# An attention block whose value products run for two key tiles at a time

## The reference, cut to what matters

```python
h = _layernorm(x) * (1 + ca) + sa                    # x: (16, 1024, 256)
q = (h @ Wq.T).reshape(b, t, 8, 64)
kv_latent = h @ Wkv_down.T                           # (b, t, 64)
k = (kv_latent @ Wk_up.T).reshape(b, t, 8, 64)
v = (kv_latent @ Wv_up.T).reshape(b, t, 8, 64)
attn = softmax(einsum('bqhd,bkhd->bhqk', q, k) * 64 ** -0.5)
x = x + ga * (einsum('bhqk,bkhd->bqhd', attn, v) @ Wo.T)
h = _layernorm(x) * (1 + cb) + sb
x = x + gb * (h @ weight.T + pooled(h) @ disha)
```

## Time and profile before

| what | value |
|---|---|
| median of 3 runs | 3648.74 us (3648.51 to 3649.03) |
| the profiled execution | 3651.17 us, its span 3649.2 us |
| mean granted TensorE clock | 0.983 |
| PE / DVE / ACT / POOL busy | 97% / 67% / 46% / 69% |
| matmul records | 15014 |

### The profile page before, as it was taken

How to read it: one execution, slowest core, us unless ns; L and a number is a source line. 1 busy time by engine, 2 the same in 40 slices (tenths; PEclk the granted TensorE clock), 3 DMA queues, 4 the chain that set the end, 5 groups by cost and what they waited for, 6 DMA issues and landing times.

```text
span 3649.2 us, 50991 instructions
## 1 busy us (share of the span) xinstructions
PE 3530.1 (97%) x15014; PEld 1840.0 (50%) x15014; DVE 2446.3 (67%) x2846; ACT 1684.6 (46%) x3075; POOL 2515.4 (69%) x1513
## 2 busy tenths in 40 slices
PE   5999999999999999999999999999999999999997
PEld 3444555545454554545545455454555545555454
DVE  4667667676676767657676576766767667676663
ACT  1445445444454545445454354543545445454443
POOL 1677767676776767668677676866767677686775
PEclk7999999999999999999999999999999999999998
DMA  1101010010101001010010100101010010100101
GB/s 55 35 20 48 24 56 21 30 48 27 47 26 55 18 27 53 24 51 18 33 47 24 51 27 27 50 27 48 21 41 36 27 48 27 53 18 33 35 30 32
DMA packets 98076, 129.24 MB, mean 35 GB/s; under 512 B 11120, under 2 KB 62448, under 8 KB 97776
## 3 DMA queue, kind: packets, MB, share of 16 engines
q1 hardware_dynamic: 97776, 125.64, 9.9%
HBM read 41.11 MB, written 16.81 MB: 16 GB/s over the span
## 4 chain that ended last, share of the span: by engine, by line
PE 94%; DVE 3%; issue 2%; ACT 1%; POOL 0%; DMA 0%; SPq 0%; DVEq 0%; POOLq 0%; ACTq 0%
PE ps_mix L543 28%; PE ps_max L593 18%; PE ps_score L564 14%; PE ps_score L566 13%; PE ps_side_b L531 7%; PE ps_side_b L651 5%; PE ps_side_a L638 4%; PE ps_side_b L669 3%; PE ps_side_a L631 1%; PE ps_side_a L658 1%; DVE h_lo L972 1%; PE ps_side_a L608 0%; DVE recip L931 0%; DVE neg_max L950 0%; PE ps_side_a L622 0%
## 5 line engine op out<-in xcount | busy, mean ns | idle before, releaser
L811 POOL TENSOR_TENSOR prob_sum<-prob_sum,probs 128x1024 f32<-128x1024 f32 x768 | 1837.5, 2393 | 575.7 <-ACT probs L710 518.7
L950 DVE TENSOR_REDUCE neg_max<-ps_max 128x1 f32<-128x1024 f32 x1016 | 1243.5, 1224 | 721.1 <-PE ps_max L593 710.9
L710 ACT ACTIVATE probs<-ps_score 128x512 f32<-128x512 f32 x2048 | 1113.0, 596 | 1140.9 <-PE ps_score L566 1129.2
L543 PE MATMUL ps_mix<-probs,values 128*64 128x512 f32 x4096 | 1109.5, 620 | 0.0
L564 PE MATMUL ps_score<-query,key_hi 128*128 128x512 f32 x2048 | 839.8, 410 | 37.2 <-issue 35.8
L566 PE MATMUL ps_score<-query_m,key_lo 128*128 128x512 f32 x2048 | 810.2, 396 | 0.0
L593 PE MATMUL ps_max<-key_hi,query 128*128 128x512 f32 x2032 | 749.8, 450 | 5.1 <-DVE neg_max L950 5.0
L593 PEld LDWEIGHTS ps_max<-key_hi,query 128*128 128x128 f32 x2032 | 304.5, 189 | 830.4 <-issue 433.6
L811 POOL TENSOR_TENSOR prob_sum<-probs 128x1024 f32<-128x1024 f32 x128 | 305.5, 2387 | 457.7 <-ACT probs L710 457.7
L931 DVE RECIPROCAL recip<-recip 128x128 f32<-128x128 f32 x512 | 481.4, 942 | 17.8 <-ACT recip L761 17.8
L564 PEld LDWEIGHTS ps_score<-query,key_hi 128*128 128x128 f32 x2048 | 387.5, 189 | 155.2 <-issue 73.9
(11 more groups left out here) (115 smaller groups left out, 2701.8 us busy)
## 6 DMA issues: line engine op xcount, KB each, us to landing
query_m<-query SPq DMA_DIRECT2D x128, 512.0 KB, 3.2
x_in<-in_L_attn_x_dram SPq DMA_DIRECT2D x16, 1024.0 KB, 5.5
x_mid<-in_L_attn_x_dram SPq DMA_DIRECT2D x64, 256.0 KB, 6.9
out_dram<-x_mid SPq DMA_DIRECT2D x64, 256.0 KB, 2.2
h_t<-gates_scratch SPq DMA_DIRECT2D x16, 256.0 KB, 6.7
query_m<-max_row SPq DMA_DIRECT2D x128, 4.0 KB
mixed<-in_L_wmod_dram SPq DMA_DIRECT2D x1, 1536.0 KB, 11.3
mixed<-in_L_attn_Wq_dram SPq DMA_DIRECT2D x1, 512.0 KB, 4.9
```

The lines of the kernel that those rows point to most:

```text
L543: last = nc.tensor.matmul(ps_mix[g % 2][j * R:j * R + R, :], values[par][:, k, :], probs[:, s % RING, j * HALF:(j + 1) * HALF], start=(k = ...
L710: nc.scalar.activation(probs[:, s % RING, half * HALF:(half + 1) * HALF], ps_score[half], ACT.Exp, scale=SCALE).then_inc(exps_done, 1)
L811: nc.gpsimd.tensor_tensor(out=total[:, :], in0=before, in1=probs[:, s % RING, :], op=ALU.add).then_inc(adds_done, 1)
L950: nc.vector.tensor_reduce(neg_max[:, m:m + 1], z.max_bank(m, ps_max, ps_scores)[:, :], AX_X, ALU.max, negate=True).then_inc(maxima_done, 1)
```

## The change

`slot` on TensorE is cut into four functions, whose bodies are the old ones, and their order is new. Even steps run the scores, the side work but for the denominator, the maximum, then the mixes of the two steps before in one block, and the denominator right behind it. Odd steps run the scores, the maximum and the side work, and no mix. The mixes of the last two steps of a batch (62 and 63) run in step 0 of the next slot. As step 0, 2, 4 and 6 of each group are even, side work at k = 0, 2, 4 and 6 now stands ahead of the maximum, and the denominator behind two mixes. The lists of the other engines are as before.

```diff
+MIXED = 2
...
-                    if s == 0 and z.has_o:
-                        if not z.has_c:
-                            need(pe, exps_done, 2 * STEPS * z.c)
-                        zo = Slot(z.o, 1 - z.par)
-                        mix(zo, STEPS - 1)
-                    if s > 0 and z.has_c:
-                        if s == 1:
-                            need(pe, a_drained, values_drained(z))
-                        mix(z, s - 1)
...
+            def side_work(z, s, denominators):
+                for kind, i, bank, b, w in z.at(s):
+                    if (kind == "denominator") != denominators:
+                        continue
...
+            def mixes(z, s):
+                if s == 0 and z.has_o:
+                    if not z.has_c:
+                        need(pe, exps_done, 2 * STEPS * z.c)
+                    zo = Slot(z.o, 1 - z.par)
+                    for t in range(STEPS - MIXED, STEPS):
+                        mix(zo, t)
+                if s > 0 and z.has_c and s % MIXED == 0:
+                    if s == MIXED:
+                        need(pe, a_drained, values_drained(z))
+                    for t in range(s - MIXED, s):
+                        mix(z, t)
...
             def slot(z):
                 for s in range(STEPS):
+                    scores(z, s)
+                    if s % MIXED == 0:
+                        side_work(z, s, denominators=False)
+                        maximum(z, s)
+                        mixes(z, s)
+                        side_work(z, s, denominators=True)
+                    else:
+                        maximum(z, s)
+                        side_work(z, s, denominators=False)
```

More of the change, by code:

```diff
@@ L547, in mix, with scores @@
                     last.then_inc(group_done, 1)
+            def scores(z, s):
+                g, k = divmod(s, NT)
+                if z.has_c:
+                    if k == 0:
+                        need(pe, max_row_set, 16 * (GROUPS * z.c + g + 1))
+                    if s == 0:
+                        need(pe, key_row_set, 16 * (z.c + 1))
+                        if isinstance(z.c, int) and z.c == 0:
+                            pe.wait_ge(maxima_done, STEPS - MAX_LAG)
+                    for j in range(2):
+                        need(pe, exps_done, 2 * (STEPS * z.c + s) - 1 + j)
+                        nc.tensor.matmul(ps_score[j], key_hi[z.par][:, k * P:(k + 1) * P],
+                                         group_queries(g)[:, j, :], start=True, stop=False)
+                        nc.tensor.matmul(ps_score[j], key_lo[z.par][:, k * P:(k + 1) * P],
+                                         query_m[:, g % 2, j * HALF:(j + 1) * HALF],
+                                         start=False, stop=True).then_inc(scores_ready, 1)
@@ new lines, in maximum @@
+            def maximum(z, s):
+                item = z.max_item(s)
+                if item:
+                    b, m = item
+                    gm, unit = divmod(m, NT)
+                    hm, qt = 2 * (gm // 2) + unit // 4, 4 * (gm % 2) + unit % 4
+                    kpar = (1 - z.par) if s >= MAX_LAG else z.par
+                    if m % (2 * NT) == 0:
+                        made = ("query", gm + 1)
+                        here = made in [p[2:4] for p in z.lists[1] if (p[4] == 0) == (s < MAX_LAG)]
+                        need(pe, b_drained, z.through(1, *made) + 1 if here else z.before(1))
+                    need(pe, maxima_done, STEPS * b + m - (0 if z.has_c else 1))
+                    bank = z.max_bank(m, ps_max, ps_scores)
+                    for half in range(2):
+                        last = nc.tensor.matmul(bank[:, half * HALF:(half + 1) * HALF],
+                                                query[:, hm, qt * P:(qt + 1) * P],
+                                                key_hi[kpar][:, half * HALF:(half + 1) * HALF],
+                                                start=True, stop=True)
+                    last.then_inc(max_scores_ready, 1)
@@ L549, in slot @@
             def slot(z):
                 for s in range(STEPS):
[L551 to L568, removed]
@@ L569, in slot @@
-                    if s == 0 and z.has_o:
-                        if not z.has_c:
-                            need(pe, exps_done, 2 * STEPS * z.c)
-                        zo = Slot(z.o, 1 - z.par)
-                        mix(zo, STEPS - 1)
-                    if s > 0 and z.has_c:
-                        if s == 1:
-                            need(pe, a_drained, values_drained(z))
-                        mix(z, s - 1)
[L579 to L663, removed]
-                            need(pe, b_drained, count)
-                            products = [(hp, wp, f) for f in range(NF)
-                                        for hp, wp in ((h2_hi, w_ffn_hi), (h2_lo, w_ffn_hi), (h2_hi, w_ffn_lo))]
-                            for j in range(CT):
-                                for q, (hp, wp, f) in enumerate(products):
-                                    last = nc.tensor.matmul(side[:, j * D:(j + 1) * D], hp[:, f, j * P:(j + 1) * P],
-                                                            wp[:, f, :], start=(q == 0), stop=(q == len(products) - 1))
-                        last.then_inc(full[bank], 1)
```

70 lines of the change are left out of this document (added).

## The result

The changed kernel takes 3990.9 us (3984.6 to 3994.8, 4 runs) against 3648.9 us (3648.5 to 3655.0): ratio 1.093, 95% interval 1.091 to 1.095. It is slower, as forecast, by 342 us where 297 were forecast; the time lies inside the range. The profiled execution took 3994.8 us.

The account below looks back on a forecast made before the run. TensorE's list, busy 97% of the span, sets the time. 3651.2 - 226 (merges) + 239 (3 to 4) + 59 + 34 (bare pairs) + 166 (ffn) + 25 (latent) = 3948 us profiled, 3946 median, 8% slower; range 3840 to 4030.

Parts of the forecast that it names:

- The saving: TensorE's mixes and denominators run in blocks: each merge saves 0.355 us, 638 merges, 226 us, 6.2%.
- 3 to 4: Maximum 4 waits for ScalarE's copies, VectorE's subtraction and reduction until D + 4.70 (D: denominator's end): 1.87 us, 236 us in all.
- The ffn: At k = 0 the ffn waits for `h2_lo` until m + 4.07 (m: maximum 7's start): 2.76 us, 60 places, 166 us.
- the lock: VectorE's `h2_lo` subtraction and GpSimd's addition of step 7 exclude each other: ffn wait 2.76 us, without it 1.98.
- The rival that the subtraction is not held: VectorE's subtraction for `h2_lo` isn't held by GpSimd's addition: 47 us less, 3899 us; chance 0.12.
- The bare pairs: Odd to even maximum without side work between stalls 0.66 us: 5 to 6 (59 us, covered groups included), 7 to 0 (34 us).
- a round trip of 1.95: From a maximum's first matmul through VectorE's reduction and semaphore, until TensorE may start the next maximum: 1.95 us.
- group 1: At maximum 5 to 6, `norm_t` in both steps waits for ScalarE's two copies: some 1.4 us a batch.
- The latent: Step 18's scores and query wait for VectorE's `key_lo`: 2.4 us less a 0.8 us wait, 25 us over 15 batches.
- the falling clock: Rival: the clock falls in the new pauses, 1.4 us at each of the 60 longest, 84 us more, 4030 us; chance 0.08.
- The signs in start distances: Mixes and denominators 0.43 us a pass; L761 starts 0.2 us behind the denominator, L950 of k = 3 ends 4.65 us behind.
- three signs of being wrong: L593 waits at k = 4 under 1 us, a mix in a block under 0.85 us, or granted clock below 0.97.

Follow-up runs that it names:

- e1: Against the kernel before: one mix a step as before, only the denominator put right behind the mix at k = 2, ahead of the maximum; 3615.6 us.
- e4: Against the changed kernel: ScalarE runs the two query copies of k = 2 ahead of the denominator's copy, TensorE's list unchanged; 3798.7 us.
- e3: Against the changed kernel: the ffn of k = 0 runs behind the pair of mixes instead of ahead of the maximum; 3828.6 us.
- e8: Against the changed kernel: GpSimd starts the addition of step 7 only after `h2_lo` is made, in groups with an ffn; 3891.6 us.
- e9: Changed kernel's order, ScalarE's query copies first, pairs of mixes only at k = 2 and 4 of groups 4 to 7, elsewhere one mix a step; 3567.4 us.
- e6: Changed kernel's order, ScalarE's query copies first, pairs of mixes only at k = 2 of seven groups (not step 18), elsewhere one mix a step; 3604.6 us.
- e7: As e6, with a second pair of mixes at k = 4 in seven groups; 3589.3 us.

## Why the prediction was right, and where it was off

- *The saving.* 0.355 us a merge: 1.77 us for two mixes in the profile after, and 0.34 us in e1. Right.
- *3 to 4.* The chain came link by link (D + 4.63 for D + 4.70), and e4 shows that it is this chain: 192 us measured. The forecast of 217 for that edit, the term of 236 less its remainder, was 13% above it.
- *The ffn.* Start at m + 4.01 for m + 4.07; e3 and e8 show both parts of the price, `h2_lo` behind maximum 7 and the addition that holds it. Without the lock the forecast would have been 47 us lower. The rival that the subtraction is not held falls.
- *The bare pairs.* 1.94 us from maximum 5 to 6 (2008.29 to 2010.23) where a round trip of 1.95 was forecast; the timeline has it so in all 31 such places of groups 0 and 7, and 1.94 to 2.03 us in 45 of the 52 bare ones from 7 to 0 (most of the others span the back edge). A bare pair of steps takes 5.50 us where it took 5.20, and with the 0.355 saved that is the 0.66 of the forecast. Only in group 1 was the term too high, by some 0.5 us a batch.
- *The latent.* 40.5 us of wait for `key_lo` in 16 places, 2.5 us each, less the 11.4 us that went: 29 for 25. The clock behind these pauses comes on top, see the sum.
- *The sum.* 45 us too low. The step that failed is the choice among the rivals: I took the falling clock for a case of its own, all 60 places or none, against a forecast with a steady clock. It fell behind 30 of the 60 pauses, 46 us. That this is the whole difference is luck, since two more errors cancel. They come out of the distances from maximum to maximum, taken step by step from both timelines for the 15 batches after the first. Where no stretch of low clock touches them their medians add up to 258 us more than before, and the forecast's terms to about 288 for the same batches (297 less 9 for the first): the steady part was some 30 us too high. The largest piece is the ffn, where a place costs 2.42 us and not 2.76, because the ffn behind the maximum already cost 0.2 us more before than it does ahead of it; 0.34 x 60 = 20 us. And the distances that low clock touches hold 92 us more than those medians, against 2 before (back edge left out): 46 behind the ffn's pauses, 27 in steps 17 to 20, most of it behind the wait for `key_lo`, 10 at k = 4 and 9 at k = 0 behind the back edge. So the clock cost twice what the ffn's places show.
- *What would show it.* I wrote that busy time would fall by 220 us and that L593's wait for L950 would be some 330 us; they were 31 and 89. Both were signs taken from sums of start distances and looked for in modelled busy times; the waits are split between the maximum, the scores ahead of it and longer-looking matmuls. The signs in start distances all came. Of the three signs of being wrong two came by their letter: the profile's wait of the maximum at k = 4 is 0.53 us, under 1 us, and the granted clock is 0.963, below 0.97. The first was a bad sign, since the stall by start distances is there; the second was a real miss, the clock above.

## What to carry to other kernels

When the engine that sets the time gets a new order, its own sum is the easy part. Write down, for each single buffer, the distance between its writes before and after, and for each engine behind it what stands ahead in its list: here the short distance was 1.4 us against a round trip of 1.95, and one copy in the wrong place of ScalarE's list cost 192 us. Batch narrow products where side work covers the step that loses them, and leave the others alone: e9 has a quarter of the changed kernel's pairs of this kind and is the fastest. And when two sums agree to a few us, add them up place by place before calling the difference explained.

## What the hardware showed that I had not expected

- The clock fell behind 30 of 60 pauses of 2.41 us and behind none of 60 of 1.62 us, in a kernel where TensorE is busy 88% of the span. A fallen clock cost 1.55 us each time, up to the scores behind the next block of mixes. In e4, which leaves these pauses as they are, it fell behind 28 of 60.
- A wait added to GpSimd made the kernel 99 us faster: its 2.4 us addition of two operands in SBUF had held up a 0.68 us subtraction on VectorE, with TensorE waiting behind that.
- The pause at the loop's back edge, about 6 us in the kernel before and in e6, was 3.6 to 3.7 us in e7 and e9 (mean of six), though e6 and e7 run the same instructions in the same order in the steps at the edge. No run shows the cause. Over six turns that is 14 us, nearly all that e7 gained over e6.
